# Layer norms' normalising and the cast of split states on ScalarE, rope halves joined in one GpSimd operation, first full scores on four row groups

## The reference

```python
def _layer(x, wqkv, qs, ksc, wo, lg, lb, w1, b1, w2, b2):   # twice in each ffn network
    h = shift_token(x)                                      # upper 64 channels one token later
    q, k, v = jnp.split(h @ wqkv, 3, axis=-1)               # 8 heads of 64
    q, k = l2norm(q) * qs, l2norm(k) * ksc
    q, k = rotary_xpos(q, k)                                # t*cos*scale + rotate_half(t)*sin*scale
    o = local_attention(q, k, v)                            # windows of 64, own and previous window
    x = x + o @ wo
    h = shift_token(x)
    h = (h - h.mean(-1)) / jnp.sqrt(h.var(-1) + 1e-05) * lg + lb
    a, g = jnp.split(h @ w1 + b1, 2, axis=-1)
    x = x + (a * gelu(g)) @ w2 + b2
def attn(x, ...):                                           # 16 heads of 8, causal softmax over 256
    q, k, v = x @ Wq + bq, x @ Wk + bk, x @ Wv + bv
    ...
```

## Time and profile before

| what | value |
|---|---|
| median of 3 runs | 1801.35 us (1790.93 to 1801.44) |
| profiled execution | 1793.28 us, its span 1791.4 us |
| PE busy | 1562.1 us, 87% |
| DVE busy | 1448.5 us, 81% |
| ACT busy | 1311.4 us, 73% |
| POOL busy | 1303.5 us, 73% |
| granted clock of TensorE, mean | 0.948 |

### The profile page before, as it was taken

How to read it: one execution, slowest core, us unless ns; L and a number is a source line. 1 busy time by engine, 2 the same in 40 slices (tenths; PEclk the granted TensorE clock), 3 DMA queues, 4 the chain that set the end, 5 groups by cost and what they waited for, 6 DMA issues and landing times.

```text
span 1791.4 us, 48412 instructions
## 1 busy us (share of the span) xinstructions
PE 1562.1 (87%) x17754; PEld 1259.1 (70%) x17754; DVE 1448.5 (81%) x2953; ACT 1311.4 (73%) x3846; POOL 1303.5 (73%) x1562
## 2 busy tenths in 40 slices
PE   3789799898988899887989899998889988898987
PEld 3667677666767777766767777776667777677776
DVE  6778789777877889877887998886788897687895
ACT  2588687667677888686779886766578877587885
POOL 7899857368648988687699997732489785469891
PEclk9799999889989999998999998997899999799999
DMA  5001101202010111111010111020210101100000
GB/s 154 16 20 28 42 23 49 92 11 60 13 49 19 25 30 49 33 25 51 24 27 19 25 27 49 21 91 26 71 26 19 52 19 55 51 22 22 19 23 13
DMA packets 49346, 66.75 MB, mean 37 GB/s; under 512 B 8114, under 2 KB 32220, under 8 KB 49116
## 3 DMA queue, kind: packets, MB, share of 16 engines
q1 hardware_dynamic: 49116, 63.66, 12.6%
HBM read 22.75 MB, written 15.73 MB: 21 GB/s over the span
## 4 chain that ended last, share of the span: by engine, by line
POOL 30%; DVE 22%; PE 21%; ACT 11%; DMA 7%; issue 7%; SPq 2%; POOLq 0%; ACTq 0%; DVEq 0%
POOL sums L1198 10%; POOL parts L1188 8%; POOL parts L1202 7%; ACT probs L1264 6%; DVE parts L1568 6%; DMA laid_dram<-halves 4%; PE bank L1640 4%; PE bank L1827 3%; DVE neg_full L1447 3%; DMA stacked_k<-laid_dram 3%; PE bank L1690 2%; PE bank L1788 2%; DVE sums L1575 2%; PE bank L1872 2%; POOL sums L1195 2%
## 5 line engine op out<-in xcount | busy, mean ns | idle before, releaser
L1188 POOL TENSOR_TENSOR parts<-parts 128x256 f32<-128x256 f32 x512 | 382.6, 772 | 136.2 <-DVE parts L1568 134.8
L1198 POOL TENSOR_TENSOR sums<-sums,neg_half 128x8 f32<-128x8 f32 x256 | 434.3, 1696 | 21.3
L1264 ACT ACTIVATE probs<-bank,neg_max 128x128 f32<-128x128 f32 x1024 | 366.2, 406 | 56.4 <-DVE neg_max L1447 54.5
L1568 DVE TENSOR_TENSOR parts<-bank,rope 128x1024 f32<-128x1024 f32 x256 | 309.0, 1216 | 48.3 <-ACT squares L1322 46.7
L1202 POOL TENSOR_TENSOR parts<-parts,sums 128x512 f32<-128x512 f32 x256 | 280.1, 1094 | 37.3 <-POOL sums L1198 0.9
L1264 ACT ACTIVATION_READ_ACCUMULATOR probs<-bank,neg_max 128x1 f32 x1024 | 249.9, 246 | 0.0
L1872 PE MATMUL bank<-ident,parts 128*128 128x128 f32 x1024 | 163.9, 284 | 67.2 <-POOL parts L1202 64.5
L1322 ACT ACTIVATE squares<-bank 128x512 f32<-128x512 f32 x256 | 158.8, 624 | 64.3 <-PE bank L1640 39.2
L1872 PEld LDWEIGHTS bank<-ident,parts 128*128 128x128 f32 x1024 | 117.4, 144 | 99.8 <-issue 71.8
L1640 PE MATMUL bank<-wqkv_hi,h_hi 128*128 128x512 f32 x384 | 179.3, 467 | 4.0 <-ACT q_t L1340 0.8
L1447 DVE TENSOR_REDUCE neg_max<-bank 128x4 f32<-128x512 f32 x256 | 164.2, 681 | 20.6 <-PE bank L1711 19.9
(11 more groups left out here) (146 smaller groups left out, 3902.6 us busy)
## 6 DMA issues: line engine op xcount, KB each, us to landing
between<-val SPq DMA_DIRECT2D x192, 128.0 KB, 2.3
laid_dram<-halves SPq DMA_DIRECT2D x96, 128.0 KB
stacked_q<-laid_dram SPq DMA_DIRECT2D x16, 512.0 KB, 3.2
stacked_k<-laid_dram SPq DMA_DIRECT2D x16, 512.0 KB, 4.3
x_sb<-in_L_attn_x_dram SPq DMA_DIRECT2D x16, 128.0 KB, 2.5
out_dram<-x_sb SPq DMA_DIRECT2D x16, 128.0 KB, 1.8
raw_qkv<-in_L_ffn_wqkv_dram SPq DMA_DIRECT2D x2, 768.0 KB, 4.7
laid_dram<-plain SPq DMA_DIRECT2D x8, 128.0 KB
```

Of the source, the lines that this page charges most:

```text
L1188: last = nc.gpsimd.tensor_tensor(joined[:, :, dst], joined[:, :, dst], sines[:, :, src], ALU.add)
L1198: nc.gpsimd.tensor_tensor(sums[:, u], sums[:, u], neg_half[:], ALU.pow).then_inc(sems["pool_step"], 1)
L1264: last = nc.scalar.activation(probs[:, u, block:block + wide].rearrange("p b j -> p (b j)"), bank[:, at:at + P * wide], ACT.Exp, bias=neg_ ...
L1568: nc.vector.tensor_tensor(parts[:, u].rearrange("p o (h d) -> p o h d", d=LOCAL_D), bank[:].rearrange("p (o h d) -> p o h d", o=1, d=LOCAL ...
```

## The change

NORM moves from DVE to ACT: one `activation` per tile with `rstd` as scale and minus mean times `rstd` as bias. POOL makes that bias, with two more instructions per layer norm. The cast of SPLIT moves to ACT. `rope_join` becomes one instruction of 512 elements whose second operand is read with the two halves of each head in reverse order. A step of S in full attention fills four banks from all four row groups, three steps a sequence instead of six; E stays as it is. The planner gets new durations, new due tables with a due time of its own for some 270 steps (`NUDGE`), `SCORES_AHEAD` 5 instead of 3, and its estimate for the way through DRAM (`SPREADING`) 14.5 instead of 9.5. At the start, DVE clears buffers instead of POOL, the masks are made in two steps, and loads and casts of the first weights go by thirds (q, k, v). The read back of `stacked_q` waits for the writes of q alone.

```diff
-SCORES_AHEAD = 3
+SCORES_AHEAD = 5
...
-    "SPLIT": [(DVE, 0.85)], "WO": [(PE, 1.75), (DVE, 0.88)],
-    "LNH": [(PE, 0.24), (DVE, 0.69), (POOL, 1.04)], "LNX": [(DVE, 0.7), (POOL, 1.06)], "NORM": [(DVE, 0.68)],
+    "SPLIT": [(ACTE, 0.27), (DVE, 0.47)], "WO": [(PE, 1.65), (DVE, 0.88)],
+    "LNH": [(PE, 0.24), (DVE, 0.69), (POOL, 1.55)], "LNX": [(DVE, 0.7), (POOL, 1.57)], "NORM": [(ACTE, 0.72)],
...
-SPREADING = 9.5
+SPREADING = 14.5
-START_AT = (-104.0, -157.6, -467.3, 8.3, -200.4, 40.8, 308.1, 166.4, 1111.4, 1166.3, 859.6, 1184.0, 826.5, 949.6,
+START_AT = (-129.0, -139.8, -451.6, -232.7, 26.0, 10.7, 168.9, 313.8, 1124.7, 1144.1, 819.3, 808.1, 1148.5, 945.6,
+NUDGE = {('E', 2, 5, 2): -15.07, ('E', 5, 5, 3): 13.11, ('E', 6, 5, 2): -2.86, ('E', 7, 5, 3): -93.87, ('E', 12, 5,
...
+    if is_full(ph) and kind == "S":
+        return [("X", s, ph, 3 * u + n) for u in range(UNIT)]
...
+            load_x(0)
+            load_qkv(0)
+            load_x(1)
...
             def norm_scale(step):
                 s = step[1]
                 pool.wait_ge(sems["var_ready"], count("var_ready", step))
+                nc.gpsimd.tensor_scalar(shift[s][:], mean_var[s][:, :, 0], -1.0, None, ALU.mult)
                 nc.gpsimd.tensor_scalar(var_eps[s][:], mean_var[s][:, :, 1], EPS, None, ALU.add).then_inc(sems["pool_step"], 1)
+                pool.wait_ge(sems["pool_step"], count("pool_step", step, 1))
+                nc.gpsimd.tensor_tensor(rstd[s][:], var_eps[s][:], neg_half[:, 0:TILES], ALU.pow).then_inc(sems["pool_step"], 1)
                 pool.wait_ge(sems["pool_step"], count("pool_step", step))
-                nc.gpsimd.tensor_tensor(rstd[s][:], var_eps[s][:], neg_half[:, 0:TILES], ALU.pow).then_inc(sems["rstd_ready"], 1)
+                nc.gpsimd.tensor_tensor(shift[s][:], shift[s][:], rstd[s][:], ALU.mult).then_inc(sems["rstd_ready"], 1)
...
-                for half in range(2):
-                    dst, src = slice(hd * half, hd * (half + 1)), slice(hd * (1 - half), hd * (2 - half))
-                    last = nc.gpsimd.tensor_tensor(joined[:, :, dst], joined[:, :, dst], sines[:, :, src], ALU.add)
-                last.then_inc(sems["rope_joined"], 1)
+                joined = parts[:, u, 0].rearrange("p (h o d) -> p h o d", o=2, d=LOCAL_D // 2)
+                sines = parts[:, u, 1].rearrange("p (h o d) -> p h o d", o=2, d=LOCAL_D // 2)
+                nc.gpsimd.tensor_tensor(joined, joined, sines[:, :, ::-1], ALU.add).then_inc(sems["rope_joined"], 1)
...
+            def split_state(step):
+                ...
+                nc.scalar.activation(h_hi[SPLIT_OF[step]][:], state[s][:, 0:T], ACT.Copy).then_inc(sems["high_ready"], 1)
+            def normalise(step):
+                s, before = step[1], last_step({"LNH", "LNX"}, step)
+                act.wait_ge(sems["rstd_ready"], count("rstd_ready", before))
+                for t in range(TILES):
+                    source = banks[BANK_OF[before]][:, P * t:P * (t + 1)] if before[0] == "LNH" else x_sb[s][:, t]
+                    last = nc.scalar.activation(normal[s][:, t], source, ACT.Identity, bias=shift[s][:, t:t + 1],
+                                                scale=rstd[s][:, t:t + 1])
+                last.then_inc(sems["normed"], 1)
...
-                    pair, of = n // 3, n % 3
+                    first, of = 2 * (n // 3), n % 3
...
-                            rows = slice(PAD_D * (2 * pair + odd), PAD_D * (2 * pair + odd + 1))
+                            rows = slice(PAD_D * (first + odd), PAD_D * (first + odd + 1))
```

More of the change, by code:

```diff
@@ new lines, with come @@
+STORING = 6.5
+PIECE_LASTS = {"table": 0.95, "w1_scaled": 0.6, "w1_hi": 0.6, "w1_lo": 0.85, "wf_scaled": 0.4, "wf_hi": 0.5, "wf_lo": 0.7}
+PIECE_COMES = {("q_hi", 0): 6.0, ("k_hi", 0): 9.0, ("v_hi", 0): 9.5, ("table", 0): 9.0, ("q_hi", 1): 20.0, ("k_hi", 1): 20.0,
+               ("v_hi", 1): 20.0, ("wf_scaled", 0): 31.0}
+X_COMES = (5.0, 6.0, 9.5, 10.0, 10.5, 11.0, 11.5, 12.0)
+def come(step, part):
+    kind, s, ph, n = step
+    if part == 0 and kind == "LNX" and ph == 0 and s < STREAMS:
+        return X_COMES[s]
+    if kind == "READY":
+        return PIECE_COMES.get(PIECES[n], 0.0)
+    if kind == "FOLD":
+        return 31.0 if n == LAYERS else 25.0 if part else 15.0
+    return 0.0
@@ L213, in passes @@
     if kind == "READY":
-        return [(DVE, PIECE_LASTS[PIECES[n][0]])]
+        what = PIECES[n][0]
+        return [(DVE, PIECE_LASTS.get(what, 0.47 if what.endswith("hi") else 0.63))]
     if kind == "FOLD":
@@ L217, in passes @@
     if kind == "MASKS":
-        return [(POOL, 5.4)]
+        return [(POOL, 3.8 if n else 5.4)]
     if kind in ("S", "E"):
-        return [(PE, (0.7 if n % 3 else 0.85) if is_full(ph) else 1.15)]
+        return [(PE, 1.23 if not is_full(ph) else (0.88 if n else 1.25) if kind == "S" else (0.7 if n % 3 else 0.97))]
     if kind == "X":
@@ L332, in weights_of @@
         what, m = PIECES[n]
-        before = {"qkv_lo": "qkv_hi", "w1_hi": "w1_scaled", "w1_lo": "w1_hi", "wf_hi": "wf_scaled", "wf_lo": "wf_hi"}
-        if what in before:
-            return made((before[what], m))
+        name, half = what.split("_") if "_" in what else (what, "")
+        if half == "lo":
+            return made((name + "_hi", m))
+        if half == "hi" and name not in QKV:
+            return made((name + "_scaled", m))
         if what == "table" and m > 0:
@@ L346, in wait @@
         after.setdefault((step, part), []).append((other, other_part % len(passes(other)), more))
-    masks = ("MASKS", 0, 0, 0)
-    after[masks, 0] = []
+    masks = [("MASKS", 0, 0, n) for n in range(2)]
+    for x in masks:
+        after[x, 0] = []
     for n, (what, m) in enumerate(PIECES):
@@ L394, in needs @@
             if is_full(ph):
-                for n in range(6):
+                for n in range(3):
                     x = ("S", s, ph, n)
-                    wait(x, 0, masks)
+                    wait(x, 0, masks[1])
                     wait(x, 0, ("QF", s, ph - 1, 0), more=SPREADING)
@@ L425, in needs @@
                 x = ("S", s, ph, u)
-                wait(x, 0, masks)
+                wait(x, 0, masks[0])
                 for y in back:
@@ L644, in lay_out @@
                     continue
-                ready = max([got[0], COME.get((x[0], x[3], part), 0.0)] + [done[b[:2]] + b[2] + handover(engine_of(*b[:2]), engine) for b in after[x, part]])
+                ready = max([got[0], come(x, part)] + [done[b[:2]] + b[2] + handover(engine_of(*b[:2]), engine) for b in after[x, part]])
                 change = CHANGE[engine] if setting(x, part) not in (None, now.get(engine)) else 0.0
@@ L700, in due_dates @@
     return {(x, part): START_AT[x[1]] + STRETCH * lone[(x[0], 0) + x[2:], part] +
-            DUE.get((x[0], part, is_full(x[2])), 0.0) + PHASE_DUE.get(x[2], 0.0) + LATER.get(x[1:3], 0.0) for x, part in after}
+            DUE.get((x[0], part, is_full(x[2])), 0.0) + PHASE_DUE.get(x[2], 0.0) + LATER.get(x[1:3], 0.0) + NUDGE.get(x, 0.0)
+            for x, part in after}
 PE_BUSY, ACT_BUSY, DVE_BUSY, POOL_BUSY = range(4)
@@ L850 @@
 PE_NEEDS, ACT_NEEDS, DVE_NEEDS, POOL_NEEDS = (first_needed(order) for order in (PE_ORDER, ACT_ORDER, DVE_ORDER, POOL_ORDER))
-FIRST_SCORED = [x for x, _ in PE_ORDER if x[0] == "S"][0]
+FIRST_MASKED = [[x for x, _ in PE_ORDER if x[0] == "S" and is_full(x[2]) == full][0] for full in (False, True)]
 FIRST_OUTPUT = [x for x, _ in PE_ORDER if x[0] == "WO"][0]
@@ L1234, in take @@
                 if step[0] == "MASKS":
-                    make_masks()
+                    make_masks_full() if step[3] else make_masks_local()
                 elif step[0] == "XB":
```

229 lines of the change are left out of this document (121 added, 108 removed), and 118 rows, old and new, of tables (DUE, LATER, NUDGE).

## The result

| | before | after |
|---|---|---|
| median | 1801.11 us (1790.93 to 1801.44, 4 runs) | 1745.32 us (1738.98 to 1747.41, 4 runs) |
| profiled execution, its span | 1793.28, 1791.4 us | 1745.73, 1743.9 us |
| PE busy; standing | 1562.1; 229.3 us | 1513.4; 230.5 us |
| mean granted clock | 0.948 | 0.964 |

The ratio is 0.9698, 95% interval 0.9655 to 0.974: 3.0% faster, 56 us by the medians. I had forecast 1712, within 1658 to 1785. The sign and the range held; the sum was 85 us, and the profiled executions differ by 47.5.

A forecast was written before the change was run, and what follows sets the result against it. No engine was full, but PE was nearest (1562.1 of 1791.4 us busy), so its work and waits counted most. Terms -25 - 37 - 15 + 5 + 15 - 20 - 8 gave -85 us: forecast 1712 us, range 1658 to 1785.

The forecast's parts named there:

- PE busy near 1500: Sign for the work taken off PE: its busy time would fall from 1562.1 us to about 1500.
- the matmuls of S below 40 us: Sign in full attention: busy time of S matmuls falls from 60.8 us; staying at 60 means four groups gained nothing.
- Four row groups: S matmuls in full attention: four row groups side by side instead of two take 25 us off PE, bounds 0 to 30.
- Shape changes: PE's list: 250 fewer changes of the array's shape at 0.15 us each save 37 us, bounds 22 to 68.
- Rope join: POOL's rope: one instruction of 1.094 us replaces two of 0.772; PE's waits shrink 15 us, bounds 0 to 27.
- Normalising and POOL's two instructions: Layer norm: two more POOL instructions cost 5 us; normalising and cast moved from DVE to ACT cost 15 us.
- The way through DRAM: PE's 41.9 us of waits for `stacked_k`: the new order and earlier read of `stacked_q` take away 20 us.
- Start: Kernel start: clearings and half the masks leave POOL's way before the first normalising, saving 8 us, bounds 0 to 10.
- B: Rival: S steps needing four free banks each wait for one more DVE maximum, 33 us, giving 1745; chance 0.10.
- D: Rival, slower: ACT stands 1.54 us for POOL at every norm, 172 us in all, giving 1864; chance 0.07.
- C: Rival, no change: PE has 60 us less work and 60 us more standing, POOL setting the pace; 1795, chance 0.09.
- A: Rival: new due times balance the engines better than the parts sum to, PE 0.93 busy, giving 1650; chance 0.14.

## Why the prediction was right in sign and too large

My sum had 62 us of work off PE and 23 us less standing. Measured in the profiles, the work fell by 48.7 us and the standing rose by 1.2. Of the signs that I named, PE busy near 1500 (1513.4) and the matmuls of S below 40 us (27.7) came true. But the same code in the old order has both in good part and gains 3 us, so they are not by themselves what made the time. By the steps of the sum:

- **Four row groups (-25).** The step holds as to PE's work: four groups do run side by side, and the matmuls of S gave 33.1 us. Their mask, of which I expected nothing, gave 11.7.
- **Shape changes (-37).** 250 fewer came, and all other matmuls together gave 3.9 us. Even with the mask's 11.7, outside the matmuls of S at most 16 us of PE's busy time can be theirs. The price of 0.15 us each was too high; 0.06 is the most that these groups allow.
- **Rope join (-15).** The bound from the scaling was too low: 1.32 us, not 1.09. Worth 11 us in the new order, nothing measurable in the old. POOL's wait did not come near the 50 us that I named; it rose to 84.5.
- **Normalising and POOL's two instructions (+20 with the cast).** The sign holds for the normalising (+7); the cast is a gain of 9. Together -2, not +20.
- **The way through DRAM (-20).** The wait went almost entirely. In the old order it is gone too, at 1797, and PE stands longer there than before. I subtracted PE's waits one by one, as if the work behind a wait removed did not meet the next one. Of all steps this one failed most plainly.
- **Start (-8).** The first normalising came at 11.4 us and PE's first matmul at 12.4 instead of 18.4, which made 4 us of work by 60 us. In the old order PE has even 6.8 us more done by then (33.26 against 26.51), at 1797. The place of the masks is worth nothing.
- **The rivals.** B is refuted: 2.5 us for maxima. That the time came out at B's 1745 is a coincidence. D priced the move at 152 us more; undoing it gave back 7, and whether they were ACT's wait for POOL (56.7 us) or POOL's own two instructions is not separated. C wanted PE to stand 60 us longer; it stands 1.2 longer, so C is wrong for the changed kernel, but it comes nearer to the parts in the old order (18.2 us less work, 23.3 more standing). A was not reached.

Two slips stand in the working: POOL and DVE have 52% of the chain, not 51, and my own bounds add up to 1784 and 1644, not 1770 and 1660. Neither moves the range that I gave.

The sign and the range were in part luck. The new order went into the sum only as fewer shape changes, and 222 of those 250 are there in the old order too. The 52 us between the two orders were in no term of mine; the terms for waits, which I had too high, covered for them.

So what I had not seen is how much lies in the order. The same code makes 1797 or 1745 us. Between these two (profiled) PE is busy 30.5 us less and stands 22.1 less: 1543.9 of 1796.5 against 1513.4 of 1743.9. No single place explains it. By the starts of the matmuls in the traces, PE has begun half of them at 905 us in the changed kernel, at 915 with the old tables and at 931 in the kernel before, and nine tenths at 1571, 1607 and 1617: the lead grows to the end. Which of the due times do this was not separated.

## What to carry to other kernels

Where a fixed order feeds in-order engines, count removed waits at little until the rows show what is late next, and do not count work off the fullest engine in full either: here 42 us off PE's S steps gave 3 us until the order was made anew. Test the order and the parts apart, both ways: the parts in the old order gave 3 us of 55 and the order with the wider steps 42. When a wait is put down to a name that the waiting code does not wait for, read the timeline around it. A move between engines has to be tried one operation at a time: of two moves from DVE to ACT one gained 9 us and one lost 7.

## What the runs showed of the hardware

- **Four row groups run side by side.** Float32 matmuls of 32 rows and 128 columns: a step of 8 from two row groups took 0.66 us, of 16 from four 0.67, and 0.69 when issued pair by pair, the second pair starting 26 ns after the first.
- **Time and granted clock go together within one kernel.** Over 33 executions of the kernel before:

```
mean clock 0.949             5 runs   1788.4 to 1796.2 us
mean clock 0.945 to 0.948   12 runs   1788.7 to 1801.8 us
mean clock 0.942 to 0.944   11 runs   1797.7 to 1803.7 us
mean clock 0.939 to 0.941    5 runs   1802.7 to 1807.1 us
a line through all 33: 13.4 us less per 0.01 of clock
```

  Twelve more, measured last, give 11.8 us less per 0.01. The slope does not carry over to another kernel. The changed code in the old order had 0.953 to 0.962 where before had 0.944 on average, and took 3 us less, not 14 to 16. With the normalising back on DVE the clock was lower (0.958 to 0.963) than in the changed kernel (0.962 to 0.971), and the time was lower too. So no share of the 55 us is put down to the clock; no run here set it by itself.
- **A GpSimd sum with one operand's halves reversed** costs 1.32 us for 128x512, where the scaling by a broadcast operand costs 1.08.
- **An activation of 128x128 with pointers for scale and bias** took 0.462 us from PSUM and 0.507 from SBUF; DVE's subtract-and-multiply took 0.402 and 0.454.
